# Cross-attention: value projections packed into odd pairs, attention outputs copied to SBUF before the reciprocal, last pair's sums on two engines

## The reference, cut to what matters

```
q = x @ Wq1
k = concat(x @ Wk1, ctx @ Wk2)      # 4352 keys
v = concat(x @ Wv1, ctx @ Wv2)
sim = einsum('bihd,bjhd->bhij', q, k) * 64 ** -0.5
out = einsum('bhij,bjhd->bihd', softmax(sim), v)
x = x + out @ Wo + bo
```

## Time and profile before

| | |
|---|---|
| median of 3 runs | 1646.91 us (1642.55 to 1647.23) |
| the profiled execution | 1643.33 us |
| its span | 1641.8 us |
| PE busy | 1449.9 us (88%) |
| POOL busy | 1049.4 us (64%) |
| DVE busy | 1124.3 us (68%) |
| ACT busy | 728.3 us (44%) |
| mean granted TensorE clock | 0.962 of full speed |

### The profile page before, as it was taken

The page is one execution under the profiler, slowest core; times in us unless marked ns, Lnnn a source line. Parts: engine busy times, 40 slices in busy tenths (PEclk is TensorE's granted clock), DMA queues, the critical chain, the costliest instruction groups (busy, mean ns, idle before and its releaser), DMA issues. The chain is left out here.

```text
span 1641.8 us, 27858 instructions
## 1 busy us (share of the span) xinstructions
PE 1449.9 (88%) x10964; PEld 1068.2 (65%) x10964; DVE 1124.3 (68%) x1299; ACT 728.3 (44%) x971; POOL 1049.4 (64%) x541
## 2 busy tenths in 40 slices
PE   4999999999999999999999999996597777827995
PEld 4767766776776776677677667664354444517995
DVE  2797578658658756855875785684776999644663
ACT  3454445534444544443554344342345333224773
POOL 3385469838547864754885665477134999443885
PEclk8999999999999999999999999998798999958998
DMA  5000021000003000001200000000304800092333
GB/s 176 14 11 11 1 87 49 1 14 21 2 27 88 24 2 14 21 1 39 88 11 14 10 11 1 1 2 1 85 19 190 214 0 1 1 368 62 63 60 59
DMA packets 62382, 76.39 MB, mean 47 GB/s; under 512 B 6384, under 2 KB 47984, under 8 KB 61856
## 3 DMA queue, kind: packets, MB, share of 16 engines
q1 hardware_dynamic: 57168, 68.51, 13.7%
q0 software_dynamic: 5088, 6.11, 2.5%
HBM read 58.39 MB, written 17.25 MB: 46 GB/s over the span
## 5 line engine op out<-in xcount | busy, mean ns | idle before, releaser
L393 POOL TENSOR_TENSOR xa_prob_sum<-xa_prob_sum,xa_probs 128x1024 f32<-128x1024 f32 x240 | 573.5, 2389 | 177.9 <-ACT xa_probs L481 158.7
L552 DVE TENSOR_REDUCE xa_maxes<-psum 128x2 f32<-128x1024 f32 (+1 forms) x288 | 334.2, 1162 | 240.1 <-PE psum L753 238.3
L481 ACT ACTIVATE xa_probs<-xa_probs 128x1024 f32<-128x1024 f32 x272 | 288.6, 1061 | 429.1 <-DVE xa_probs L574 428.8
L574 DVE TENSOR_TENSOR xa_probs<-psum,xa_max_rows 128x1024 f32<-128x1024 f32 x272 | 330.3, 1216 | 14.8 <-PE psum L784 8.5
L796 PE MATMUL psum<-xa_probs,xa_vals 128*64 128x256 f32 x2176 | 280.9, 389 | 4.0 <-ACT xa_probs L481 2.8
L796 PEld LDWEIGHTS psum<-xa_probs,xa_vals 128*64 128x64 f32 x2176 | 137.8, 136 | 106.4 <-issue 42.9
L780 PE MATMUL psum<-xa_q_hi,xa_k_hi 64*128 64x256 f32 x1088 | 158.8, 285 | 0.8 <-DVE xa_probs L574 0.8
L678 PE MATMUL psum<-xa_wv_hi,xa_ctx_hi 128*128 128x256 f32 x512 | 150.9, 295 | 7.8 <-DVE xa_maxes L552 7.8
L784 PE MATMUL psum<-xa_q_hi,xa_k_lo 64*128 64x256 f32 x1088 | 155.3, 279 | 0.0
L782 PE MATMUL psum<-xa_q_lo,xa_k_hi 64*128 64x256 f32 x1088 | 155.2, 279 | 0.0
L753 PE MATMUL psum<-xa_k_hi,xa_q_hi 64*128 64x512 f32 (+1 forms) x604 | 136.0, 452 | 21.4 <-DVE xa_maxes L552 9.3
(11 more groups left out here) (329 smaller groups left out, 2887.0 us busy)
## 6 DMA issues: line engine op xcount, KB each, us to landing
xa_ctx_in<-in_ctxT_dram SPq DMA_DIRECT2D x32, 512.0 KB, 4.6
ex_slots<-mx_blank_tile SPq DMA_DIRECT2D x2, 4372.5 KB, 38.4
xa_stage<-in_L_xattn_Wk_dram SPq DMA_DIRECT2D x32, 128.0 KB, 2.4
xa_stage<-in_L_xattn_Wv_dram SPq DMA_DIRECT2D x16, 256.0 KB, 3.0
ex_raw<-in_L_ffn_w_gate_dram SPq DMA_DIRECT2D x8, 512.0 KB
ex_raw<-in_L_ffn_w_up_dram SPq DMA_DIRECT2D x8, 512.0 KB
ex_raw<-in_L_ffn_w_down_dram SPq DMA_DIRECT2D x8, 512.0 KB
ex_xt<-ex_slots SPq DMA_DIRECT2D x15, 265.0 KB, 3.1
```

Source lines behind the costliest of these rows:

```text
L393: pool.tensor_tensor(prob_sum[:, :], prob_sum[:, :], probs[:, n % RING, :], ALU.add).then_inc(summed, 1)
L481: nc.scalar.activation(probs[:, n % RING, :], probs[:, n % RING, :], ACT.Exp, scale=HD ** -0.5).then_inc(exp_done, 1)
L552: dve.tensor_reduce(maxes[:, qt, :, g:g + 1], max_banks(v, g, qt)[:, :, 0:group_keys(g)[1]], AX_X, ALU.max).then_inc(max_reduced, 1)
L574: dve.tensor_tensor(probs[:, n % RING, :].rearrange("p (h t q) -> p h t q", h=2, t=2), S[:, 2 * (n % 2):2 * (n % 2) + 2, :].rearrange("p h ...
```

## The change

1. Values: during odd u tiles 0 to 15 in steps 1 to 8, two a step; in the even pair only tile 16, in step 0. In odd pairs the order on PE is now: both weighings, then the values, then the next keys. In step 8 the values stand ahead of the last weighing. DVE splits a group of keys in odd pairs (and in step 1 of even ones) between the first reduction and the first shift of the next step.
2. Outputs: `sum_probs` moves ahead of the keys in step 0; ACT copies the whole bank O (outputs and sums, 512 columns) to SBUF (`raw`). The next pair's first weighing waits for this copy (`o_stored`). Reciprocal and multiplication then read SBUF, in step 0 of even pairs, in steps 1 and 2 of odd ones. The last pair keeps PSUM as source.
3. The last pair: the tiles with j % 3 == 1 (1, 4, 7, 10, 13, 16) are added by DVE into `late_sum`, the others by POOL; PE sums both over the partitions.
4. `store_k_hi(v, 1)` stands behind the second exponential in step 0; ACT's and DVE's order at a pair's end changes a little (`store_q_hi` and `split_q` come earlier). `ones` is 128x64 f32.

```diff
+def late(j):
+    return j % 3 == 1
...
         def v_due(u, d):
             if u % 2 == 1 and u + 1 < U:
-                return [((u + 1) // 2, j) for j in (2 * d - 4, 2 * d - 3) if 0 <= j]
+                return [((u + 1) // 2, j) for j in (2 * d - 2, 2 * d - 1) if 0 <= j]
             if u % 2 == 0 and u > 0:
-                return [(u // 2, j) for j in (2 * d + 14, 2 * d + 15) if j < HG]
+                return [(u // 2, HG - 1)] if d == 0 else []
...
# ScalarE
+            def store_outputs(u):
+                act.wait_ge(sums_ready, u + 1)
+                act.wait_ge(pv_done, (u + 1) * HG)
+                if u > 0:
+                    act.wait_ge(o_normalized, u)
+                nc.scalar.activation(raw[:, :, :].rearrange("p a q -> p (a q)"), O, ACT.Copy).then_inc(o_stored, 1)
+                if d == 0:
+                    if following:
+                        store_k_hi(v, 0)
...
+                    exponentials(u, 0)
+                    if u > 0:
+                        store_outputs(u - 1)
+                    if chunk is not None:
+                        split_chunk(u // PAIRS + 1, chunk)
+                    exponentials(u, 1)
+                    for c, j in v_due(u, d):
+                        store_values(c, j)
+                    if following:
+                        store_k_hi(v, 1)
...
# VectorE
             def invert_sums(u):
+                else:
+                    dve.wait_ge(o_stored, u + 1)
+                    dve.reciprocal(raw[:, 1, :], raw[:, 1, :]).then_inc(sums_inverted, 1)
...
-                dve.tensor_tensor(heads_T[:, p, :], O[:, 0:N1], inv_sum[:, :], ALU.mult).then_inc(o_normalized, 1)
+                dve.tensor_tensor(heads_T[:, p, :], O[:, 0:N1] if u == U - 1 else raw[:, 0, :], raw[:, 1, :],
+                                  ALU.mult).then_inc(o_normalized, 1)
+            def add_late(j):
+                n = (U - 1) * HG + j
+                dve.wait_ge(exp_done, n + 1)
+                if j == 1:
+                    dve.tensor_copy(late_sum, probs[:, n % RING, :]).then_inc(late_summed, 1)
+                else:
+                    dve.wait_ge(late_summed, late_done(j) - 1)
+                    dve.tensor_tensor(late_sum, late_sum, probs[:, n % RING, :], ALU.add).then_inc(late_summed, 1)
...
                     shift(u, 1)
+                    if u > 0 and u % 2 == 0:
+                        invert_sums(u - 1)
+                        normalize(u - 1)
                     continue
+                if following:
                     reduce_max(v, d - 1, 1)
-                if d == 1 and u > 0:
-                    invert_sums(u - 1)
-                    normalize(u - 1)
+                    if u % 2 == 1 or d == 1:
+                        split_keys(v, d)
                 shift(u, 2 * d)
+                if following:
                     reduce_max(v, d, 0)
...
                     shift(u, 2 * d + 1)
+                    if u % 2 == 1 and d == 1:
+                        invert_sums(u - 1)
+                    if u % 2 == 1 and d == (2 if following else 1):
+                        normalize(u - 1)
+                    if following and u % 2 == 0:
                         split_keys(v, d + 1)
...
+                if not following:
+                    for j in (2 * d - 2, 2 * d - 1):
+                        if late(j):
+                            add_late(j)
+            add_late(HG - 1)
...
# TensorE
-                    pe.wait_ge(o_normalized, u)
+                    pe.wait_ge(o_stored, u)
...
+                if following and d == 0:
                     score_for_max(v, d, 0, values)
+                    if u > 0:
+                        sum_probs(u - 1)
+                    for c, j in v_due(u, d):
+                        project_values(c, j, maxima)
+                        values += 1
                     project_keys(v, d + 1, maxima, values)
+                elif following and d < STEPS - 1:
+                    score_for_max(v, d, 0, values)
+                    if u % 2 == 0:
+                        if d == 2 and u > 0 and u % PAIRS == 0:
+                            project_output(u // PAIRS - 1)
+                        project_keys(v, d + 1, maxima, values)
+                    for j in weighed:
                         weigh(u, j)
                     for c, j in v_due(u, d):
                         project_values(c, j, maxima)
                         values += 1
+                    if u % 2 == 1:
+                        project_keys(v, d + 1, maxima, values)
```

More of the change, by code:

```diff
@@ L65, in step_tiles, with late_done @@
     return [j for j in (2 * d, 2 * d + 1) if 0 <= j < HG]
+def late(j):
+    return j % 3 == 1
 def sums_done(n):
-    return n // HG * (HG - 1) + max(1, n % HG)
+    u, j = n // HG, n % HG
+    if u == U - 1:
+        return u * (HG - 1) + max(1, sum(not late(i) for i in range(j + 1)) - 1)
+    return u * (HG - 1) + max(1, j)
+def late_done(j):
+    return sum(late(i) for i in range(j + 1))
 def group_keys(g):
@@ L153, in sem @@
             return sems[-1]
-        ones = sb("xa_ones", [P, P], F32R)
+        ones = sb("xa_ones", [P, HD])
         ctx_hi = sb("xa_ctx_hi", [P, DC, N2], F32R)
@@ L409, in _ @@
             for u, d in steps():
-                if d >= 1:
+                if d >= 1 and not (u == U - 1 and late(2 * d - 1)):
                     add_probs(u, 2 * d - 1)
@@ L413, in _ @@
                     split_weights(u + 2)
-                if d >= 1:
+                if d >= 1 and not (u == U - 1 and late(2 * d)):
                     add_probs(u, 2 * d)
@@ L505, in _ @@
                 v = u + 1
[L506 to L509, removed]
-                exponentials(u, 2 * d)
-                if d + 1 < NG and v < U:
-                    store_k_hi(v, d + 1)
-                if d < STEPS - 1:
-                    exponentials(u, 2 * d + 1)
-                for c, j in v_due(u, d):
-                    store_values(c, j)
+                following = v < U
@@ new lines, in _ @@
+                chunk = chunk_due(u, d)
+                if d == 0:
+                    if following:
+                        store_k_hi(v, 0)
+                        if own_due(u, d) is not None:
+                            store_own_hi(own_due(u, d))
+                    exponentials(u, 0)
[8 more added lines that the diff above has]
+                        store_k_hi(v, 1)
+                    continue
@@ new lines, in _ @@
+                exponentials(u, 2 * d)
+                if d == STEPS - 1:
+                    if u + 2 < U:
+                        store_q_hi(u + 2)
+                    for c, j in v_due(u, d):
+                        store_values(c, j)
+                    if chunk is not None:
+                        split_chunk(u // PAIRS + 1, chunk)
+                    if u + 2 < U:
+                        split_weights(u + 2)
+                    continue
+                if u % 2 == 0:
+                    if following:
+                        store_k_hi(v, d + 1)
+                    exponentials(u, 2 * d + 1)
+                    if chunk is not None:
+                        split_chunk(u // PAIRS + 1, chunk)
+                else:
+                    if chunk is not None:
+                        split_chunk(u // PAIRS + 1, chunk)
+                    exponentials(u, 2 * d + 1)
+                    for c, j in v_due(u, d):
+                        store_values(c, j)
+                    if following:
+                        store_k_hi(v, d + 1)
@@ L801, in sum_probs @@
             def sum_probs(u):
[L802 to L807, removed]
+                if u == U - 1:
+                    parts = (late_sum, prob_sum)
+                    pe.wait_ge(late_summed, late_done(HG - 1))
+                else:
+                    parts = (prob_sum,)
+                for k, part in enumerate(parts):
+                    if part is prob_sum:
+                        pe.wait_ge(summed, sums_done((u + 1) * HG - 1))
+                    for t in range(2):
+                        for h in range(2):
+                            i = pe.matmul(O[half[h], N1:2 * N1], ones[:, :],
+                                          part[:, (2 * h + t) * N1:(2 * h + t + 1) * N1],
+                                          start=(k == 0 and t == 0), stop=(k == len(parts) - 1 and t == 1))
                 i.then_inc(sums_ready, 1)
@@ L891, in _ @@
                         values += 1
+                    weigh(u, HG - 1)
                     turn_maxima(v, values)
```

56 lines of the change are left out of this document (25 added, 31 removed).

## The result

The changed kernel takes 1637.63 us (median; 1634.91 to 1639.55) where the kernel before takes 1646.97 in the same comparison: the ratio is 0.9948, with an interval of 0.9924 to 0.9973. That is a gain of 0.5%.

The account below looks back on a forecast made before the run. PE's own work was taken to set the pace. Odd pairs +3.6, even -4.0, with extras for u % 4 = 3 and pair 0, sum to 0; the last pair gives -7.3: 1640 from the median, range 1624 to 1650.

Parts of the forecast that it names:

- +4.6 for a new wait of the values on DVE: Odd pairs: values wait for the reduction of the step's first maxima, beginning 0.66 late in seven steps, +4.6 a pair.
- Rival 2: Odd steps: the values' wait is hidden, DVE's chain being ready at T + 4.2; 32 more gained, 1608; chance 0.08.
- The term of +0.7 for u % 4 = 3: Three odd pairs: the copy of keys 1 stands behind an exponential and a chunk on ACT, +0.7 each.
- The -1.1 for the wait of step 2: Odd pairs, step 2: the wait goes because shift 4 no longer stands behind the reciprocal, -1.1 a pair.
- The +1.0 for the multiplication: Even pairs: DVE's multiplication stands still until POOL's first add ends, delaying step 1's reduction, +1.0; range 0 to 1.4.
- a -0.1 of which it gives no source: Even pairs: an unexplained -0.1 in the sum that comes to -4.0 a pair.
- 0.7 was forecast: Pair 0: it makes no values, and only its copy of keys 1 is later, +0.7.
- the chain followed: Last pair: DVE's and POOL's adds, each waiting for the other's running instruction, followed to a reciprocal at 1135.8, -6.4.
- The -0.9 for clock and projection: End of the last pair: with a shorter hole ahead the clock may hold, and the output projection gains too, -0.9.
- the -6.4: Last pair: the reciprocal comes at 1135.8 instead of 1142.15, with the sum's 16 matmuls taking 2.1.
- The holding up of both engines: Last pair: DVE's and POOL's adds exclude each other; the reciprocal gains 6.4 where it would gain 10.5 if nothing blocked.

Follow-up runs that it names:

- Part 3 alone: Kernel before with only the last pair's sums split over two engines (tiles with j % 3 == 1 added by VectorE): 1640.76 us, ratio 0.9960.
- part 2 alone: Kernel before with only the outputs copied to SBUF by ScalarE and the reciprocal and multiplication later on VectorE: 1630.05 us, ratio 0.9911.

## Why the prediction was right

**Odd pairs.** They grew by 3.4 where 3.6 was forecast. The term that decided it, +4.6 for a new wait of the values on DVE, was right in place (304.75 = T + 4.88) and size (0.63 against 0.66 in this step). That it is the split's place in the chain, and no matter of DVE's load, is shown from both sides: 0.60 less in the chain gives 0.61 less a step, and 0.60 more gives 0.60 more. Rival 2 described the kernel with the later split: 1608 was worked out for a hidden wait, and 1605.8 was measured once it was.

The term of +0.7 for u % 4 = 3 measured 0.67, but only in part for the reason given. 0.4 of it comes ahead of the copy of keys 1: POOL's last add of the pair before ends late in these three pairs, and `sum_probs`, which now stands ahead of the keys, waits 0.32 for it and starts 0.39 later than in the others. The prediction had read this wait as 0.2 at u = 3 and counted nothing for it. The chunk and the late copy of keys 1, to which it gave all 0.7, are left with 0.28, and cost nothing once the split had moved. That this term came out is partly luck.

The -1.1 for the wait of step 2 was put down to the late reciprocal alone. The outputs by themselves bring only 0.4 an odd pair; the rest needs the new order of part 1.

**Even pairs.** They lost 4.05 to 4.5 where 4.0 was forecast. The +1.0 for the multiplication was measured as 1.03. (The prediction's sum holds a -0.1 of which it gives no source.) The pairs u = 2, 6 and 10 gain 0.45 more than reckoned; with the outputs alone all even pairs gain the same 1.15, so it comes with the other parts, and more was not found.

The Trainium skill (SBUF — State Buffer, Who interferes with whom) has it that a VectorE instruction with two SBUF inputs and a GpSimd instruction that reads SBUF exclude each other for the whole instruction. The trace agrees: the multiplication of 0.42 becomes 2.16 beside an add of 2.40, and 1.22 becomes 2.42 in the last pair.

**Pair 0.** It grew by 1.3 where 0.7 was forecast. In the kernel after the granted clock was below full at its start; with tile 15 moved, where pair 0 is the same code at full clock, it takes 52.19, which is +0.45. The other kernels bear this out: at a clock of 1.00 in its first 5 us pair 0 takes 52.16 to 52.19 in all four, and at 0.91, 0.87 and 0.79 it takes 52.62, 52.80 and 53.16. In these windows (of the kernel after, its first 5 us, then of that with tile 15 moved) the number behind POOL's is the granted clock:

```profile
78.00:83.00 5.00, 5.00 (x41) 4.10 (x39) 3.51 (x5) 2.73 (x3) 3.31 (x5) 0.80 0.17 57
```

```profile
76.00:81.00 5.00, 5.00 (x54) 4.20 (x54) 4.29 (x6) 2.91 (x4) 4.07 (x6) 1.00 0.28 93
```

**Last pair.** It lost 6.9 where 7.3 was forecast, but by other terms, so that the closeness is partly luck. The reciprocal gained 6.9 and not 6.4: the chain followed had POOL's add of tile 15 go ahead of DVE's add of tile 16. It was the other way round, DVE's add at 1128.40 was not held up, and half of the sum (1129.67) ran while POOL finished. The -0.9 for clock and projection did not come. The sum's eight matmuls took 1.08, at full clock, but the -6.4 had them so already (16 in 2.1); and the projection behind took 2.08 as before, at a granted clock of 0.50. Over the kernels tried here it was 1.13 with tile 15 moved, 1.62 without POOL's adds and 2.01 to 2.08 in most others, behind the same hole of 2.32. What decides it is open. The holding up of both engines was put at 4.1 in the time of the reciprocal, and there it measured 4.2.

**Each part by itself.** Part 3 alone takes 6.9 from the last pair, as much as the whole change does. In pairs 0 to 14 part 2 alone brings 10.7 (1016.7 to 1006.0), but the whole change only 2.6 (1014.1). So parts 1 and 4, as written, cost about 8 there, and the kernel gains in spite of them. With the split one place later these pairs take 982.7, and the two parts bring 23 instead. (By the medians of whole kernels part 2 alone brings 15 and the whole change 9.3, so the cost is no smaller by these.)

## What to carry to other kernels

An engine with free time can still be the one that is waited for: list the instructions between the event that it waits for and the one for which the bottleneck waits, and put behind that chain what is not needed in it. When work that covered a wait is moved, write down the time at which each side is ready (T + 4.22 and T + 4.88 here): the difference times the number of steps is the price, and the edit that removes it can be read off the same chain. A sum shared between DVE and POOL is not halved in time when both read SBUF (POOL's adds and what they held up still cost 4.2 here). Giving tile 15, one of the last pieces, to the faster engine and summing first the part that was ready first brought 1.05. And look where each part of a sum was measured: a term can come out right for two reasons, of which only one was forecast.

## What was not expected of the hardware

A VectorE copy with one SBUF input (0.68 alone) was held by POOL's add just like the adds with two inputs (2.85). The prediction had let it wait in its chain, but its rows and its rule spoke of two inputs only. The reciprocal from SBUF to SBUF, beside the same kind of add, was not held (1.741 to 1.744 in 15 of 15). An instruction that was held ran nearly its own length once POOL's add had ended: the multiplication (0.42) ended 0.28 after it in all 15 cases of the kernel after, the copy (0.68) 0.55, the two adds (1.22) 1.08. So being held costs what is left of POOL's add, less 0.14. The output projection's four matmuls took anything from 1.13 (nearly all at the 2.4 GHz level, granted 0.92) to 2.08 (at 1.2 GHz, granted 0.50) behind the same hole of 2.32, in kernels in which the eight matmuls of the sum ahead of it took 1.03 to 1.08 at a granted clock of 1.00.
